# A convolution as three half filters over even and odd columns, with part of the tap sums added on VectorE

## The reference, cut to what matters

```python
x = L0_attn_a_x                                   # (2, 512, 256) float32: batch, channel, column
def _L0_attn_a_ref(x, block_values, cols, rows):  # block_values (128, 64, 64, 16)
    xb = x.reshape(batch, n_block_row, bs, t)     # 8 blocks of 64 channels
    x_unfold = xb[:, cols].reshape(batch, n_blocks * bs, t)
    W = block_values.reshape(n_blocks * bs, bs, ks)
    o = jax.lax.conv_general_dilated(x_unfold, W, window_strides=(1,), padding=[(ks - 1, 0)],
        dimension_numbers=('NCH', 'OIH', 'NCH'), feature_group_count=n_blocks)
    y = jnp.zeros((batch, n_block_row, bs, t), o.dtype).at[:, rows].add(o.reshape(...))
x = x + _L0_attn_a_ref(_layernorm(x, axis=-1), block_values, cols, rows)
x = x + _L0_ffn_ref(_layernorm(x, axis=-1), ...)
```

## Time and profile before

| what | value |
|---|---|
| median of 3 runs | 873.48 us (873.46 to 874.2) |
| span of the profiled execution | 873.0 us |
| PE busy | 865.5 us (99%) |
| DVE, ACT, POOL busy | 501.8, 420.0, 320.0 us |
| chain that ended last | PE 93%, DVE 3%, ACT 1%, DMA 1% |

### The profile page before, as it was taken

The page is one execution under the profiler, slowest core; times in us unless marked ns, Lnnn a source line. Parts: engine busy times, 40 slices in busy tenths (PEclk is TensorE's granted clock), DMA queues, the critical chain, the costliest instruction groups (busy, mean ns, idle before and its releaser), DMA issues.

```text
span 873.0 us, 16737 instructions
## 1 busy us (share of the span) xinstructions
PE 865.5 (99%) x5617; PEld 773.3 (89%) x5620; DVE 501.8 (57%) x1360; ACT 420.0 (48%) x978; POOL 320.0 (37%) x293
## 2 busy tenths in 40 slices
PE   9999999999999999999999999999999999999998
PEld 7999878888888888889989998998997888888887
DVE  4777757333333338887688668768877433333334
ACT  3522416334334344776377557647746433434332
POOL 5211014556555564232121213212112556556552
PEclk9999999999999999999999999999999999999999
DMA  8999312111111102000000100000002111111111
GB/s 338 362 383 391 136 40 77 49 54 36 54 45 45 54 18 76 1 26 21 18 3 21 36 0 24 0 0 1 1 1 73 38 54 39 51 54 36 54 36 49
DMA packets 25554, 61.01 MB, mean 70 GB/s; under 512 B 3298, under 2 KB 10916, under 8 KB 25508
## 3 DMA queue, kind: packets, MB, share of 16 engines
q1 hardware_dynamic: 23204, 47.82, 16.1%
q0 software_dynamic: 2304, 12.58, 3.8%
HBM read 59.35 MB, written 1.05 MB: 69 GB/s over the span
## 4 chain that ended last, share of the span: by engine, by line
PE 93%; DVE 3%; ACT 1%; DMA 1%; issue 1%; POOL 0%; DVEq 0%; ACTq 0%
PE bank L1131 29%; PE bank L1655 25%; PE bank L1144 14%; PE bank L534 7%; PE bank L545 5%; PE bank L1781 4%; PE bank L1721 3%; PE bank L1157 2%; PE bank L1167 2%; DMA cv_shared<-in_wtaps 1%; PE bank L1746 1%; DVE cv_acc L421 1%; PE bank L518 1%; PE bank L1675 1%; PE bank L129 0%
## 5 line engine op out<-in xcount | busy, mean ns | idle before, releaser
L1030 DVE TENSOR_TENSOR f_h<-f_scaled,bank 128x512 f32<-128x512 f32 (+1 forms) x90 | 60.8, 676 | 179.4 <-POOL f_scaled L895 166.9
L812 ACT ACTIVATE f_h_hi<-f_h 128x512 fp32r<-128x512 f32 (+2 forms) x102 | 63.6, 624 | 186.2 <-DVE f_h L1030 186.0
L895 POOL TENSOR_TENSOR f_scaled<-f_act,f_gate_rows 128x512 f32<-128x512 f32 x80 | 102.9, 1287 | 116.3 <-ACT f_act L805 115.9
L1131 PE MATMUL bank<-f_xt_hi,f_w_lo 128*128 128x512 f32 x352 | 138.2, 393 | 0.0
L1131 PE MATMUL bank<-f_xt_hi,f_w_hi 128*128 128x512 f32 x352 | 137.8, 391 | 0.0
L1350 ACT ACTIVATE at_prob<-bank,at_sbias,at_qrs 128x512 f32<-128x512 f32 (+3 forms) x128 | 77.6, 618 | 72.6 <-DVE at_sbias L1542 72.6
L1037 DVE TENSOR_TENSOR f_h_lo<-f_h,f_h_hi 128x512 fp32r<-128x512 f32 (+2 forms) x102 | 71.8, 704 | 70.7 <-ACT f_h_hi L812 70.4
L1131 PE MATMUL bank<-f_xt_lo,f_w_hi 128*128 128x512 f32 x352 | 108.8, 390 | 0.0
L1144 PE MATMUL bank<-f_w_lo,f_h_hi 128*128 128x256 f32 (+1 forms) x352 | 99.6, 283 | 0.0
L1144 PE MATMUL bank<-f_w_hi,f_h_lo 128*128 128x256 f32 (+1 forms) x352 | 99.6, 283 | 0.0
L1144 PE MATMUL bank<-f_w_hi,f_h_hi 128*128 128x256 f32 (+1 forms) x352 | 99.3, 282 | 0.0
(11 more groups left out here) (232 smaller groups left out, 2062.8 us busy)
## 6 DMA issues: line engine op xcount, KB each, us to landing
cv_raw<-in_wconv SPq DMA_DIRECT2D x26, 512.0 KB, 6.7
cv_shared<-in_wtaps POOLq DMA_DIRECT2D x16, 768.0 KB, 7.7
f_wraw<-in_w SPq DMA_DIRECT2D x42, 256.0 KB, 2.6
xn<-in_wconv SPq DMA_DIRECT2D x14, 512.0 KB, 6.5
f_wraw<-in_w SPq DMA_DIRECT2D x42, 128.0 KB, 2.5
at_wraw<-in_wqkv SPq DMA_DIRECT2D x3, 768.0 KB, 4.4
at_oraw<-in_wo SPq DMA_DIRECT2D x4, 512.0 KB, 3.5
X<-in_x_tiles SPq DMA_DIRECT2D x2, 512.0 KB, 8.0
```

Of the source, the lines that this page charges most:

```text
L812: a.activation(h_hi[slot][0:rows, cols], h_f[half][0:rows, cols], ACT.Copy).then_inc(s["h_hi_done"], 1)
L895: g.tensor_tensor(scaled[half][:], act[half][:], gate_rows[:, half * HALF:(half + 1) * HALF], ALU.mult).then_inc(s["scaled_done"], 1)
L1030: v.tensor_tensor(h_f[half][0:rows, cols], src[half][0:rows, cols], pu[half][0:rows, cols], ALU.mult)\
L1131: mm = t.matmul((pg, pu)[gu][half][0:out_rows, :], w, x, start=q == 0, stop=q == 3 * KH - 1)
```

## The change

The output is computed in even and odd columns. With the input's even columns X0 and odd columns X1, three streams of 128 columns a batch are made: X0, XA (odd columns one to the left, minus X0) and XB (X1 minus X0). An output of either phase is a filter of its own with XA or XB plus a filter, the sum of the two, with X0, which both phases share. Every filter now has 8 taps (`FT`) at half the columns (`M` = 128 a batch). `TAPS` reorders the taps so that stages 0, 2, 4, 6 hold the filter of one phase and 1, 3, 5, 7 that of the other; the shared filter is `FIR` + 0 to 3, sums of the stages (0, 1), (2, 3), (4, 5), (6, 7).

- PE: 12 filters by 8 units by 3 matmuls of 256 columns, where 8 filters of 512 were. The shared results go to bank `P2_BANK` = 3, so `BANKS` is 3.
- DVE: in stages 1 and 3 an addition per bank (bank plus `full[0]` into `full[1]`) makes the shared filter; ACT rounds it (`round_pair`) and POOL makes its low part (`low_pair`).
- POOL: makes XA and XB (`differences`), copies the upper channel rows to `xp` (`upper_rows`, 8 copies), and after DVE's last block adds the last two shared filters (`added_pair_sums`, 4 additions).
- The end is 10 pieces of 12 matmuls in the order `LAST_PRODUCTS`; ACT and DVE split in the order `ADDED_ORDER`. The last row is added a batch at a time after the last piece.
- `round_input` and `split_input` handle 64x768 for 64x1024.

```diff
-        BANKS = 4
+        BANKS = 3
+        P2_BANK = 3
...
+        ADDED_ORDER = ((5, 0), (7, 0), (FIR + 2, 0), (5, 1), (FIR + 2, 1), (7, 1), (FIR + 3, 0), (6, 0), (FIR + 3, 1), (6, 1))
+        LAST_PRODUCTS = ((5, 0), (FIR + 2, 0), (FIR + 2, 1), (FIR + 3, 0), (FIR + 3, 1), (6, 0), (7, 0), (5, 1), (6, 1), (7, 1))
...
-        BANK_BLOCKS = ((5,) * 8, (5,) * 8, (6, 6, 6, 6, 6, 4, 0, 0))
+        BANK_BLOCKS = ((4,) * 8, (5,) * 8, (6, 6, 5, 5, 5, 5, 5, 5))
...
+            def round_pair(i):
+                a.wait_ge(s["pair_sums"], SB * (i + 1))
+                a.activation(ws_hi[SLOT[FIR + i]], full[1][:, 0:NLOW, :], ACT.Copy).then_inc(s["pair_hi_done"], 1)
...
+            def differences(b):
+                x = xs[b]
+                g.wait_ge(s["xn_ready"], GC * b + LG)
+                g.tensor_tensor(x[:, :, XB, :], x[:, :, X1, :], x[:, :, X0, :], ALU.subtract).then_inc(s["x_parts"], 1)
+                g.tensor_tensor(x[:, :, XA, 1:M], x[:, :, X1, 0:M - 1], x[:, :, X0, 1:M], ALU.subtract).then_inc(s["x_parts"], 1)
+                g.tensor_tensor(x[:, :, XA, 0:1], xp[:, 0:LG, b, 0:1], x[:, :, X0, 0:1], ALU.subtract).then_inc(s["x_parts"], 1)
+
+            def upper_rows(b):
+                g.wait_ge(s["xn_ready"], GC * (b + 1))
+                for k in range(2):
+                    for par in range(2):
+                        lo = KS - 1 - 2 * k
+                        g.wait_ge(s["x_parts"], 3 * B + 4 * b + 2 * k + par)
+                        g.tensor_copy(xp[k * BS:(k + 1) * BS, par::2, b, lo:lo + D], xh[b][par * BS:(par + 1) * BS, :, :])\
+                         .then_inc(s["x_parts"], 1)
...
+            def low_pair(i):
+                g.wait_ge(s["pair_hi_done"], i + 1)
+                g.tensor_tensor(ws_lo[SLOT[FIR + i]], full[1][:, 0:NLOW, :], ws_hi[SLOT[FIR + i]].bitcast(F32), ALU.subtract)\
+                 .then_inc(s["pair_lo_done"], 1)
+
+            def added_pair_sums(i, r):
+
+                other = full[0][:, 0:NLOW, :] if i == 2 else acc[:, 1, 0:NLOW, :]
+                g.tensor_tensor(row_part(low_of(FIR + i), r), row_part(acc[:, 0 if i == 2 else 2, 0:NLOW, :], r),
+                                row_part(other, r), ALU.add).then_inc(s["pair_sums"], 1)
...
+                    if st % 2:
+                        cols = slice(q * OB, (q + 1) * OB)
+                        v.tensor_tensor(full[1][:, 0:NLOW, cols],
+                                        ps[(st * SB + q) % BANKS][:].rearrange("p (w o) -> p w o", o=OB)[:, 0:NLOW, :],
+                                        full[0][:, 0:NLOW, cols], ALU.add).then_inc(s["pair_sums"], 1)
...
+            t.wait_ge(s["x_parts"], 3 * B + 4 * B)
+            for u in units(0):
+                products(*u)
```

More of the change, by code:

```diff
@@ L30 @@
 XPITCH = 272
+M = D // 2
+FT = KS // 2
+SPITCH = 136
+TAPS = [(1 - st % 2) + 4 * (st // 2) + 2 * k for st in range(NST) for k in range(2)]
 NPE, ND = 5, 3
@@ L331, in clear_sums, with powers @@
                     g.memset(acc[:, :, q * NW // ZEROED:(q + 1) * NW // ZEROED, :], 0.0).then_inc(s["acc_zeroed"], 1)
-            g.wait_ge(s["flag_ready"], 1)
-            clear_sums(range(0, 3))
-            for b in range(B):
+            def powers(b):
                 part = slice(b * GC, (b + 1) * GC)
@@ L348, in gpsimd @@
                 g.dma_start(raw_d[d % 3], ins["wtaps"][d].rearrange("p (n f) -> p n f", n=DB)).then_inc(raw_d_in[d % 3], 16)
+            def low_pair(i):
[6 more added lines that the diff above has]
+                                row_part(other, r), ALU.add).then_inc(s["pair_sums"], 1)
+            g.wait_ge(s["flag_ready"], 1)
+            clear_sums(range(0, 3))
+            powers(0)
+            g.wait_ge(s["pads_ready"], 3)
+            differences(0)
+            powers(1)
+            differences(1)
+            clear_sums(range(3, ZEROED))
+            g.wait_ge(s["rstd_ready"], B)
+            tap_blocks(0)
+            for b in range(B):
+                upper_rows(b)
+            g.wait_ge(s["x_parts"], 7 * B)
+            for d in (1, 2):
+                tap_blocks(d)
+            d = 3
+            for st in range(2, NPE):
+                for q in range(SB):
+                    while d < NDC and DB * (d - 2) <= blocks_behind(st, q):
+                        tap_blocks(d)
+                        d += 1
+                    if st % 2 == 0 and q == 1:
+                        low_pair(st // 2 - 1)
+            g.wait_ge(s["ws_hi_done"], NPE * SB)
+            g.wait_ge(s["pair_lo_done"], 2)
+            g.wait_ge(s["added"], 2 + 2 * NBLK)
+            for i in (2, 3):
+                for r in range(LG):
+                    added_pair_sums(i, r)
             first_weights["low"](g)
@@ L363, in last_rows @@
             low_half(v, 0)
[L364 to L369, removed]
-            following["statistics"](v, [following["order"].index(tile)])
-            following["variances"](v, 3)
+            for b in range(B):
+                add_phases(v, 1, GC + 1, 6 + b, slice(b, b + 1))
+                row_statistics(v, 1, (b,))
+                following["variances"](v, 2 + b)
             following["normalize"](v, 2)
```

296 lines of the change are left out of this document (166 added, 130 removed).

## The result

The changed kernel takes 914.95 us (median of 4 runs, 913.96 to 915.46) against 873.76 (4 runs beside them): 1.0469 times as long, 95% interval 1.0455 to 1.0484. The forecast was 870.3, and its slowest rival 875.6. The profiled execution took 914.75 us with a span of 913.0, against 873.0. The first row of PE with work for the second half, which the prediction computed as 127, stood at 130.21 before; it is now at 170.00. All 40 us are lost in the convolution.

The account below looks back on a forecast made before the run. Bound taken: PE's bank sums and DVE's additions, ending together near 101.6 us, DMA close. PE's 4.7 us gained less 1.5 for the last row, 3.2 net, gives 869.8 from 873.0, or 870.3 on the median; range 864 to 875.

Parts of the forecast that it names:

- Stages 2 to 4 on PE: Convolution: stage 2 takes 17.1 us, stages 3 and 4 20.0 each; PE's sums end at 96.5 without waits.
- Copies end at 36.2: Head: POOL's eight copies, 0.62 us each plus turns with DVE's splits, end at 36.2; products start at 36.5.
- rival 2: Head: POOL's copies cost 1.3 us each, end at about 41.5, everything behind comes 5.3 us later: 875.6; chance 0.15.
- POOL's subtraction holds DVE off for about its length: Stages 2 to 4: DVE stands twice for `low_pair` on POOL, 2.41 - 0.16 = 2.25 us each.
- The second load lands at about 41: Ahead of stage 2: POOL's load for DVE goes behind the copies at 36.5; DVE reaches stage 2 at 43.0 at best.
- T: The moment DVE's additions end and PE needs the first piece: 101.4 us, range 100 to 102.5.
- Pieces wait 3 us in all: The end: pieces start at 103.5, 106.9 and 109.3 behind DVE's low sums, waiting 3 us in all.
- The last row loses 1.5 us: The end: both batches of the last row are added after the last piece, cutting the gain from 4.7 to 3.2 us.
- Rival 3: The DMA is the real bound: DVE done at 103.5 instead of 101.4, 872.4, no measurable change; chance 0.2.
- Rival 1: DVE and POOL hinder each other less: copies end by 33, PE's sums bring additions' end to 98, 864.2; chance 0.2.

Follow-up runs that it names:

- e14: The changed kernel without its skipped bodies on PE, with `low_pair` and `added_pair_sums` on DVE and POOL's second load issued earlier: 871.0 us, ratio 0.997.
- e1: The changed kernel without the two skipped `t.If(flag != 0)` bodies on PE: 879.6 us, ratio 1.010.
- e9: The whole changed kernel, skipped bodies kept, plus twelve products of zeros on PE behind the first bank of stages 2 and 4: 893.3 us, ratio 1.021.
- e5: The changed kernel without its skipped bodies on PE and with `low_pair` moved from POOL to DVE: 875.6 us, ratio 1.004.

## Why the prediction was wrong

**The failed step** is that under "Stages 2 to 4 on PE": "Stages 3 and 4 have two filters, 20.0 each, what they had. Without waits the sums end at 39.4 + 57.1 = 96.5." They ended at 133.7. The sum went over the instructions that run, each at its duration from rows with a clock of 1.00. The longer `high_products`, which is part of the change though the text ahead of the prediction doesn't tell of it, had no term, since nothing of it runs; passing over it made PE stand. The two stands up to there are 6.7 of the 37 us. And no term asked what the clock does behind a stand: at 0.50 a bank took 3.4 us in place of 1.78.

**The account**, by the moment at which the second half goes on (130.21 before). The form alone, with its instructions there in time, POOL's subtractions and sums on DVE and the load early, gives -5.3 (e14, 124.95). POOL's holds, the late load and the half clock behind one wait: +9.2 (e14 to e1, 134.10). The skipped bodies: +35.9 (e1 to the changed kernel, 170.00). Sum +39.8. Of the last term e9 got 21.7 back with 13.0 of the 14.4 us of stands left in, so most of it is the clock; how it divides exactly stays open, since a stand also takes the place of a wait.

**Point by point.**
- Copies end at 36.2, filter 0 starts at 36.5, PE having waited 1 us: 36.5, 36.63 and 0.45. That is partly luck: the copies began at 27.83 for 26.1, and took 8.65 us for the 10.1 allowed; half the turns between 31.1 and 38.4, the prediction's own rule, would have given 34.8 for its 36.2. The shortest took 0.61, the price taken from the rows. With the turns they came to 1.08 on average, over the 0.9 that was named as a sign of rival 2; but they ended at 36.5 and not at 41.5, so rival 2 fell.
- POOL's subtraction holds DVE off for about its length: four additions behind 2.37 us took 3.34 for 0.77, 2.6 more. The size was near. Its effect was not: I charged it to DVE's chain; what counted was PE's wait up to 91.54, for the half clock behind it.
- The second load lands at about 41: DVE's additions went on at 44.62. Mis-sized by 3.6 us.
- T, the end of DVE's additions, 101.4: 102.45 in e5, the form with no fetch stands but `low_pair` on DVE; 106.8 in e1.
- Pieces wait 3 us in all: 2.24 in e1. The last row loses 1.5 us: in e5 the next stage starts 2.85 earlier than before and the second half 0.83, so 2.0.
- Rival 3, the DMA is the bound: the changed kernel's share of 0.70 from 43 to 80 us says only that PE was slow. In e14, with the clock at 1.00, the share is 1.01 from 35 to 90 us at about 400 GB/s, and DVE waits for loads 8 times, 5.6 us in all. So whether the DMA bounds the form without stands stays open. Rival 1, DVE and POOL hinder each other less, fell: see the four additions.
- With fetch, holds and late load out of the way the kernel is at 871.0, near my 870.3. That is other edits than the change had, and no success of the sum, which had the holds and the load in it: e1, the form as it was changed but for the bodies, is at 879.6, 9.3 over it.

## What to carry to other kernels

Count the instructions in code that is skipped, too: list each engine's instructions in order, and where some hundreds are passed over within a few microseconds, look for idle time put down to "issue" (or to a semaphore whose setter was done long before) and for instruction packets in it. Spread such code between long-lasting instructions, or make it shorter; many short pieces one behind another are worse than one jump (12.21 us for 960 instructions against 3.84 for 1280). And ask of every wait that a change may add on TensorE what runs behind it: a stand of 2.5 us cost 4.2 in all ahead of 36 products of 256 columns, while one of 2.4 ahead of banks of 64 columns left the clock at half for 37 us, and products of zeros in the idle time can be cheaper than none.

## What the runs showed of the hardware

- One packet of PE's instructions, 256 of them, takes 3.05 us when four are needed one behind another with the DMA idle; PE stood 4.24 us with one packet in them and the DMA 1.00 busy. One jump over 1280 instructions cost 3.84 us and fewer packets than it passed.
- Twenty-four added products of 512 columns of zeros made a kernel 21.7 us faster, nearly all of it by the clock: its stands were only 1.4 us shorter.
- A POOL operation that reads SBUF and DVE's additions take turns: a whole subtraction of 2.4 us is waited out by four small additions. On DVE the same subtraction let e5 run 4.0 us faster than e1.
